# A bidirectional Mamba layer on one core: scan inputs in three PSUM banks, convolution two units ahead, one list position per scan

## What is computed

```python
xz = jnp.einsum('ed,bld->bel', in_proj_w, hidden_states)
out_f = _mamba_dir(xz, ...)
out_b = _mamba_dir(xz[:, :, ::-1], ...)[:, :, ::-1]
return jnp.einsum('bdl,od->blo', out_f + out_b, out_proj_w)
...
# _mamba_dir, 256 channels d, 16 states n, 512 positions l
u = _causal_conv_silu(x, conv_w, conv_b)
x_dbl = jnp.einsum('bdl,kd->bkl', u, xproj_w)
delta = jax.nn.softplus(jnp.einsum('dr,brl->bdl', dtproj_w, x_dbl[:, :r]) + dt_bias)
dA = jnp.exp(jnp.einsum('bdl,dn->bdln', delta, A))
dBx = jnp.einsum('bdl,bnl,bdl->bdln', delta, Bm, u)
h = _ssm_scan(dA, dBx)
y = jnp.einsum('bdln,bnl->bdl', h, Cm) + Dp * u
return y * silu(z)
...
# ffn: Hadamard transform, 4-bit quantization per token, ternary weight
xq = _quantize_activations(xn @ H)
return jnp.einsum('bsi,oi->bso', xq, _ternary_quantize_ste(weight))
```

## Time and profile before

| | |
|---|---|
| runs | 977.39, 978.01, 972.45 us; median 977.39 |
| profiled execution | 976.08 us, span of its instructions 974.0 us |
| mean granted TensorE clock | 0.864 of 2.4 GHz |
| DMA | 72.5 MB, mean 74 GB/s |
| POOL, states by C | 256 times, mean 2365 ns |
| DVE, scans | 512 times, mean 1202 ns |
| ACT, decays | 512 times, mean 710 ns |

### The profile page before, as it was taken

The page is one execution under the profiler, slowest core; times in us unless marked ns, Lnnn a source line. Parts: engine busy times, 40 slices in busy tenths (PEclk is TensorE's granted clock), DMA queues, the critical chain, the costliest instruction groups (busy, mean ns, idle before and its releaser), DMA issues.

```text
span 974.0 us, 13835 instructions
## 1 busy us (share of the span) xinstructions
PE 765.9 (79%) x3873; PEld 384.4 (39%) x3873; DVE 800.2 (82%) x838; ACT 782.1 (80%) x1454; POOL 750.2 (77%) x454
## 2 busy tenths in 40 slices
PE   3486977689786977979689697878978697797994
PEld 1233443343433435334353344434443343433452
DVE  2278988898788878888888887889878887897995
ACT  2599995899878987789967998589986898878970
POOL 2159887788768977789787887878886798777994
PEclk9788988889787988979889797988978798897797
DMA  3424225070620607024070512507052070702400
GB/s 91 113 66 118 48 79 107 4 163 4 141 55 30 135 3 172 24 70 91 30 166 3 126 38 70 124 3 162 3 126 68 10 154 3 172 14 68 95 7 27
DMA packets 51433, 72.53 MB, mean 74 GB/s; under 512 B 6704, under 2 KB 19920, under 8 KB 51408
## 3 DMA queue, kind: packets, MB, share of 16 engines
q1 hardware_dynamic: 50976, 71.97, 31.6%
q10 hardware_dynamic: 432, 0.26, 0.1%
HBM read 60.68 MB, written 11.53 MB: 74 GB/s over the span
## 4 chain that ended last, share of the span: by engine, by line
POOL 29%; issue 27%; PE 18%; ACT 15%; DVE 8%; DMA 2%; POOLq 1%; SPq 0%; DVEq 0%; ACTq 0%
POOL hst L678 22%; PE pb L792 5%; DVE hst L569 5%; ACT da L416 4%; POOL dbx_t L688 4%; PE b_ps L879 4%; ACT dbx_t L405 2%; PE y L894 2%; PE b_ps L864 1%; PE y L891 1%; POOL t_log L694 1%; ACT xn L308 1%; PE pb L856 1%; DVE b_ps L557 1%; PE pb L811 1%
## 5 line engine op out<-in xcount | busy, mean ns | idle before, releaser
L678 POOL TENSOR_TENSOR hst<-hst,c_rep 128x1024 f32<-128x1024 f32 x256 | 600.6, 2365 | 170.8 <-DVE hst L569 170.1
L569 DVE TENSOR_TENSOR_SCAN hst<-da,b_ps 128x512 f32<-128x512 f32 x512 | 586.3, 1202 | 43.1 <-ACT da L416 21.4
L879 PE MATMUL b_ps<-ident,dbx_t 128*128 128x128 f32 x1536 | 246.6, 301 | 158.3 <-DVE hst L569 157.4
L416 ACT ACTIVATE da<-rep,neg_a 128x511 f32<-128x511 f32 x512 | 336.2, 710 | 5.8 <-DVE hst L569 3.8
L879 PEld LDWEIGHTS b_ps<-ident,dbx_t 128*128 128x128 f32 x1536 | 181.0, 151 | 281.2 <-DVE hst L569 255.7
L405 ACT ACTIVATE dbx_t<-du_t,b_t 128x256 f32<-128x256 f32 x576 | 247.0, 496 | 2.5 <-PE b_ps L879 1.7
L894 PE MATMUL y<-hst,sum_sel 128*32 128x512 f32 x1024 | 148.9, 657 | 3.0 <-POOL hst L678 3.0
L792 PE MATMUL pb<-xnt,conv_wt 128*128 128x512 f32 x256 | 121.0, 617 | 0.8 <-ACT xnt L316 0.8
L688 POOL TENSOR_TENSOR dbx_t<-du_t,b_t 128x1024 f32<-128x1024 f32 x48 | 91.3, 1903 | 2.7 <-ACT du_t L388 2.7
L864 PE MATMUL b_ps<-t_log,spread_sel 32*128 32x512 f32 x256 | 73.4, 679 | 14.3 <-POOL t_log L740 9.8
L557 DVE TENSOR_TENSOR b_ps<-b_ps,b_rep 128x1024 f32<-128x1024 f32 x64 | 78.0, 1219 | 5.4 <-PE b_ps L864 5.4
(11 more groups left out here) (111 smaller groups left out, 588.5 us busy)
## 6 DMA issues: line engine op xcount, KB each, us to landing
rep<-d_scr SPq DMA_DIRECT2D x128, 256.0 KB, 9.1
c_rep<-bc_scr SPq DMA_DIRECT2D x64, 256.0 KB, 4.8
d_scr<-t_pos SPq DMA_DIRECT2D x15, 512.0 KB, 3.0
b_rep<-bc_scr SPq DMA_DIRECT2D x64, 64.0 KB, 2.2
x_ln<-x SPq DMA_DIRECT2D x8, 256.0 KB, 3.3
x_res<-x SPq DMA_DIRECT2D x8, 256.0 KB, 2.8
out<-x_res SPq DMA_DIRECT2D x8, 256.0 KB, 7.1
conv_wt<-conv_w SPq DMA_DIRECT2D x2, 512.0 KB, 5.8
```

The costliest lines, as they stand in the source:

```text
L416: nc.scalar.activation(da[s % 2][:, j, 1:L], rep[d][h][:, j, 1:L], ACT.Exp, scale=neg_a[:, d, h, j, q:q + 1]).then_inc(decay_done, 1)
L569: nc.vector.tensor_tensor_scan(hst[s % RING][:, j, :], da[s % 2][:, j, :], b_ps[:, j, :], 0.0, ALU.mult, ALU.add).then_inc(scan_done, 1)
L678: nc.gpsimd.tensor_tensor(hst[s % RING][:, two, :], hst[s % RING][:, two, :], c_rep[d][:, q:q + 1, :].broadcast_to([P, 2, L]), ALU.mult).t ...
L879: ins = tr(b_ps[:, j, P * c:P * (c + 1)], dbx_t[(NX * d + q - 1) % 2][:, c, NJ * h + j, :, :].rearrange("p r e -> p (r e)"), ident[:, :])
```

## The change

- `b_ps` has three banks instead of four, and scan g (counted through all units) uses bank g mod 3; `pb` has three instead of two. PE issues the input of scan k+3 as soon as scan k is done.
- The lists of all engines go scan by scan: PE, DVE and ACT have a position per scan k, with side work behind it. Copies are issued one at a time instead of in pairs, and `times_b` works on one bank, a scan ahead.
- The convolution for W goes tap by tap behind the inputs of positions 8, 9, 10, 12 (half 0) and 16, 17, 20, 21 (half 1) of unit U. The sigmoids are at ACT's positions 17 and 27, `make_u` at DVE's 16 and 23, so u for W is made in unit U. x_proj for V is at PE's positions 0 and 1. `log_error`, `correction` and `delta` are behind scans 9, 10, 11; before, they were around scans 14 and 15.
- All batches are written out; the hardware loop and its registers are gone. The prologue makes unit 1's u and normalizes batch 1 as well.
- The quantized activations go into `x_ln` instead of `xn`, and x is loaded two batches ahead, behind the rep loads. B and C are spread before delta is stored. The token scale is computed on DVE instead of POOL; x_proj and `steps` use 64 columns or rows once; z_proj reads `xnt_kept`.

The core of the diff:

```diff
+G = NJ * SLOTS
+UNITS = 2 * NB
+BANKS = 3
+CONV_BANK = (2, 0)
...
-        b_ps = ps("b_ps", [P, NJ, L])
+        b_ps = ps("b_ps", [P, BANKS, L])
         y = ps("y", [P, NH, L])
-        pb = ps("pb", [P, 2, L])
+        pb = ps("pb", [P, 3, L])
...
             def load_x(b):
-                src = rows(x, b)
-                wait(sp, xn_ready, b)
-                sp.dma_start(x_ln[:, :, :], src).then_inc(x_loaded, DMA)
+                wait(sp, xn_ready, b - 1)
+                wait(sp, xqt_filled, b - 2)
+                sp.dma_start(x_ln[:, :, :], rows(x, b)).then_inc(x_loaded, DMA)
...
+            def spread(V):
+                d = V % 2
+                store_bc(V)
+                load_bc(V)
                 sp.wait_ge(delta_ready, V + 1)
                 sp.dma_start(d_scr[d].rearrange("h p l -> p h l"), t_pos[:, :, :]).then_inc(delta_stored, DMA)
-                load_bc(d, V)
                 sp.wait_ge(delta_stored, DMA * (V + 1))
                 for h in range(NH):
                     load_delta(d, h)
...
+            for U in range(UNITS):
+                b, d = divmod(U, 2)
+                if U < UNITS - 1:
+                    spread(U + 1)
+                if d == 0 and b + 2 < NB:
+                    load_x(b + 2)
+                if d == 1 and b > 0:
                     store_out(b - 1)
+                    load_res(b)
...
+                wait(act, scan_done, G * U + k - 2 * NJ + 1)
+                nc.scalar.activation(da[s % 2][:, j, 1:L], rep[d][h][:, j, 1:L], ACT.Exp, scale=neg_a[:, d, h, j, q:q + 1]).then_inc(decay_done, 1)
...
+                for k in range(G):
+                    decay(U, k)
...
+                    if k == 5 and nxt:
+                        keep_xdbl(V)
...
+                    if k in (8, 9) and nxt:
+                        softplus_in(V, k - 8)
+                    if k == 10 and nxt:
+                        keep_bt(V)
+                        softplus_exp(V)
+                    if k == 11 and nxt:
+                        softplus_one(V)
+                    if k == 12:
                         if nxt:
+                            softplus_log(V)
+                        if d == 1 and b + 2 < NB:
+                            log_var(b + 2)
+                            guess_rstd(b + 2)
...
+                    if k == 17:
+                        if conv:
+                            u_sigmoid(W, 0)
+                        inputs_free(U, 3, 2 * U + 2)
+                        inputs_t(U, 3, 0)
+                    if k in (18, 19, 20):
+                        inputs_t(U, 3, k - 17, whole=k == 20)
+                    if k == 22 and d == 1 and b + 2 < NB:
+                        normalize(b + 2, x_ln)
+                    if k == 23 and nxt:
+                        keep_dut(V, 0, 2 * V + 1)
+                    if k == 25 and nxt:
+                        inputs_free(V, 1, 2 * V + 1)
+                        inputs_t(V, 1, 0)
+                    if k == 26 and nxt:
+                        keep_dut(V, 1, 2 * V + 2)
+                        inputs_t(V, 1, 1)
+                    if k == 27 and conv:
+                        u_sigmoid(W, 1)
...
+                    if k + 1 < NH * NJ:
+                        times_b(U, k + 1)
+                    if k == G - 1 and nxt:
+                        times_b(V, 0)
+                    scan(U, k)
+                    if k == 2 and d == 0 and b > 0:
+                        gate_y(b - 1, 0)
+                    if k == 5 and d == 0 and b > 0:
                         gate_y(b - 1, 1)
+                    if k == 9 and nxt:
+                        log_error(V)
+                    if k == 10 and nxt:
+                        correction(V)
+                    if k == 11 and nxt:
                         delta(V)
+                    if k == 16 and conv:
+                        make_u(W, 0)
+                    if k == 20 and d == 0 and b + 2 < NB:
+                        statistics(b + 2, x_ln)
+                    if k == 23 and conv:
+                        make_u(W, 1)
...
+                wait(pe, scan_done, g - BANKS + 1)
+                mm(b_ps[:, g % BANKS, :], spread_sel[at, :], du[at, s, :], start=True, stop=True).then_inc(t_filled, 1)
...
+                    if k + BANKS < G:
+                        inputs(U, k + BANKS)
                     elif nxt:
+                        inputs(V, k + BANKS - G)
+
+                    if k in (0, 1) and nxt:
+                        pe.wait_ge(u_ready, 2 * V + 2)
+                        if d == 0:
+                            wait(pe, xq_ready, b)
                         else:
+                            pe.wait_ge(dut_ready, 2 * U + 2)
+                        x_proj(V, k)
...
+                    if k == 4 and nxt:
                         if d == 0:
+                            pe.wait_ge(xnt_ready, min(b + 2, NB))
                         else:
+                            pe.wait_ge(gate_ready, 2 * b + 2)
+                        steps(V, 0)
+                    if k == 5 and nxt:
                         if d == 0:
+                            wait(pe, xqt_ready, b)
                         else:
+                            pe.wait_ge(gate_ready, 2 * b + 1)
+                        steps(V, 1)
+                    if k == 6 and nxt:
+                        b_transposed(V, pb[:, 2, :])
+                    if k % NJ == NJ - 1 and k > NJ:
+                        sum_states(U, k // NJ - 1)
+                    if k in (8, 9, 10, 12) and conv_next:
+                        pe.wait_ge(bt_ready, V + 1)
+                        pe.wait_ge(xnt_ready, W // 2 + 1)
+                        conv(W, 0, ((8, 9, 10, 12).index(k),))
+                    if k in (13, 14):
+                        skip_product(U, k - 13)
+                    if k in (16, 17, 20, 21) and conv_next:
+                        pe.wait_ge(delta_ready, V + 1)
+                        conv(W, 1, ((16, 17, 20, 21).index(k),))
+                    if k == 18 and nxt:
+                        pe.wait_ge(delta_ready, V + 1)
+                        du_transposed(V, 0)
```

More of the change, by code:

```diff
@@ L78, in build @@
         qinv = sb("qinv", [P, NC])
-        xq = xn
+        xq = x_ln
         xqt = sb("xqt", [P, L])
@@ L178, in wait @@
         def wait(eng, s, count):
-            if not isinstance(count, int) or count > 0:
+            if count > 0:
                 eng.wait_ge(s, count)
-        def batches(eng, body):
-            body(0)
-            with eng.Fori(1, NB - 1) as i:
-                body(i)
-            body(NB - 1)
-        def first(b):
-            return isinstance(b, int) and b == 0
-        def last(b):
-            return isinstance(b, int) and b == NB - 1
         @block.sync
@@ L241, in spread @@
                     load_delta(d, h)
-            load_x(0)
+            sp.dma_start(x_ln[:, :, :], rows(x, 0)).then_inc(x_loaded, DMA)
             for d in range(2):
@@ L498, in _ @@
+            for U in range(UNITS):
+                unit(U)
             keep_xqt(NB - 1)
@@ L582, in _ @@
-            statistics(0)
+                nc.vector.tensor_tensor(x_res[:, :, :], pb[:, 1, :].rearrange("p (c o) -> p c o", c=NC), x_res[:, :, :], ALU.add).then_inc(out_ready, 1)
+            statistics(0, x_ln)
             for n in range(2):
@@ L785, in _, with conv @@
             tr = nc.tensor.transpose
-            def conv(d, V, h, taps, free, count):
-                wait(pe, free, count)
+            def conv(V, h, taps):
+                d = V % 2
                 for k in taps:
@@ new lines, in inputs, with skip_product @@
+                wait(pe, scan_done, g - BANKS + 1)
+                for c in range(NC):
+                    ins = tr(b_ps[:, g % BANKS, P * c:P * (c + 1)], dbx_t[(NX * d + q - 1) % 2][:, c, NJ * h + j, :, :].rearrange("p r e -> p (r e)"), ident[:, :])
+                ins.then_inc(t_filled, 1)
+            def skip_product(U, h):
+                d = U % 2
+                step = slice(None, None, -1 if d else 1)
+                pe.wait_ge(u_ready, 2 * U + 2)
+                mm(y[:, h, :], skip[:, d, h, :], u[d][:, h, step], start=False, stop=False, skip_group_check=True)
@@ L887, in sum_states @@
                     wait(pe, y_read, 2 * b - 1 + h)
-                if s == SKIP_AT - 1:
-                    pe.wait_ge(u_ready, 2 * (2 * b + d) + 2)
-                    for n in range(NH):
-                        mm(y[:, n, :], skip[:, d, n, :], u[d][:, n, step], start=False, stop=False, skip_group_check=True)
                 pe.wait_ge(prod_done, 2 * S + 2)
@@ L919, in _ @@
-            du_transposed(0, 1, delta_ready, 1)
-            conv(1, 1, 0, range(TAPS), dut_ready, 1)
-            conv(1, 1, 1, range(TAPS), dut_ready, 2)
+            x_proj(0, 1)
+            steps(0, 0)
+            steps(0, 1)
+            b_transposed(0, y[:, 1, :])
+            pe.wait_ge(first_du, 1)
+            for k in range(BANKS):
+                copy(0, k)
+            pe.wait_ge(delta_ready, 1)
```

(9 more changed lines are left out.)

703 lines of the change are left out of this document (313 added, 390 removed).

## The result

The changed kernel takes 1238.95 us (four runs, 1234.29 to 1241.11) against 977.67: 1.268 times as long, 95% interval 1.263 to 1.274. Forecast were 1031 us, range 968 to 1080. The direction was right, the size was not. The profiled execution has a span of 1232.7 us, at a mean granted clock of 0.75 instead of 0.864.

What follows compares the result with a forecast made beforehand. Hand-overs between engines, no engine filling the span, were taken as the bound. Start 82, intervals 7 x 58.2 and 7 x 63.6, late x 13, end 88.5, less 7 gave 1029 us, with 2.1 around it 1031; range 968 to 1080.

Steps and rivals of the forecast that it cites:

- Smaller items: Minor effects across engines: single copies, three banks and POOL's work called hidden; removed registers and branches save 0.5 us per interval.
- the sum: Whole run: start 82, seven intervals each of 58.2 and 63.6, late x 13, end 88.5, minus 7: 1029 us of span.
- first L: L is a unit's first correction of the logarithm on DVE; the run's first was placed at 82 us, before at 78.2.
- Half clock over the copies: Rival, k=0 to 5: PE idles at k=23, stays at 1.2 GHz; two steps cost 3 to 4 us a unit, 1075; chance 0.07.
- second stall at `make_u`: Behind scan 23, DVE waits for half 1's sigmoid: about 6 us in a forward unit, 8 in a backward one.
- the wait at `log_error`: DVE waits there for ACT's logarithm 4.6 us a unit instead of 2.7, about 65 us in all.
- Half 0's sigmoid: ACT sees the convolution's half 0 finished at L+9.9, after waiting 5.5 us at this first sigmoid.
- the wait for x: At k=20, statistics waits for x loaded behind the rep loads, delaying the sigmoid 2.2 us; six forward units, 13 us.
- credit of 7 us for the removed registers: Loop's register arithmetic and branches gone: 0.5 us saved per interval, 7 us in all, bounds 0 and 14.
- the faster rival: ACT reaches the second sigmoid in time, stalls at make_u sum below about 6 us a pair; 920 or 940 us; chance 0.17.
- the ring: Engines pass four moved things round each unit; ACT waits for a tap behind scan 12; intervals 58.2 and 63.6 us.
- ACT then bound by its own: Variant of the faster rival: ACT limits at 49 us a unit plus waits of 5, intervals 54 and 57, 940 us.

Runs made afterwards that it cites:

- e1: The changed kernel with du copies at full height: 128-row selection weights, zero outside the 32 rows that select, and all 128 rows of du; 1064.78 us.
- p1: A separate kernel computing nothing of the layer: PE issues nine stretches of fp32 matmuls without waits, each after a rest of about 16 us; its time is no comparison.
- e4: e1 with ACT's second sigmoid behind decay 23 instead of 27; 1059.96 us.
- e5: e4 with x of batch b+2 loaded ahead of the B, C and delta spreads instead of behind the rep loads; 1044.29 us.
- e6: e5 with log_error, correction and delta behind scans 12, 13, 14 instead of 9, 10, 11, and make_du one POOL slot later; 989.13 us.
- e11: e6 with first sigmoid and its make_u at 18, backward second du_t copy behind decay 24, softplus chain and keep_xdbl later on ACT; 943.44 us.

## Why the prediction went wrong, step by step

**The step that failed** stands under "Smaller items": "in k=0 to 5 a step is copy plus projection, 1.8, against DVE's 1.12 + 0.6 = 1.7, hidden while the clock is full". The clock is not full there: the step takes 3.9 us at 0.50, DVE waits 119.8 us for copies, and e1 shows the price, 174 us, 84% of the miss of 208. By the terms of the sum: 14 intervals of 74.8 instead of 61.3 are 189 us; first L 87.9 instead of 82 and end 97.7 instead of 88.5 are 15; in e1 these two are 82.3 and 90.3. The last 4 are the distance from the profiled execution to the median.

**The rival was on the list, but with the wrong price and cause.** "Half clock over the copies" had chance 0.07 and 3 to 4 us a unit, "two such steps". It costs 11.5 us an interval (74.8 - 63.3), and 13 us more in the beginning and the end: the low clock covers not two steps but 32 us, from the last copies of one unit over projection, sums and steps to the taps of the next. Its cause was wrong too: the prediction let the idle time at k=23 lower the clock and any work raise it again. Idle time does lower it (from the second on, each stretch of p1 starts at 0.50 behind its rest of 16 us, and 642 to 644 above is at 0.50), but it is back at 1.00 before the copies, and p1 shows matmuls that never raise it. And the evidence against it, at 560 to 562, was of transposes and state sums, which p1 shows at 1.00; it said nothing of 32-row matmuls. The window from 562 to 582 of the same trace holds 32-row copies at 1.00, but in pairs and beside taps, and single copies could not be read from it either. The Trainium skill ("TensorE: Matmul & The Clock Gate", "Part 4: PE-mode transpose") has it that the full clock does not engage for transposes; the fp32 transposes of p1, with 1.00 from 315 to 321, do not agree, and the trace decides.

**What held.** With the clock restored (e1) the sum can be judged. First L 82.3 (82), end 1058.6 - 968.3 = 90.3 (88.5), total 1064.8 (1031): 34 us off, 3%, with no term wrong by more than 4 us a unit. So the direction was not luck: with the full clock the changed kernel is still 1.091 times the one before. But the prediction put most of the loss on the second stall at `make_u`, and taking the waits away one after the other gives 5 us for that stall (e4), 16 for x (e5) and 55 for the wait at `log_error` (e6). Half 0's sigmoid starts at L+8.4 in the changed kernel (predicted 9.9; the clock was already full there), the second is done at L+26.8 (predicted 28.2, backward):

```profile
619.89 0.69 ACT L325 ACTIVATE t_exp<-pb,half_bias 128x512 f32<-128x512 f32 x1 [3.81 <-PE pb L819]
...
637.65 0.63 ACT L327 ACTIVATE t_exp<-t_exp 128x512 f32<-128x512 f32 x1
```

DVE stalls 5.75 us at `make_u` in this backward unit (8) and 6.13 in the forward unit behind it (6). The 99 us in all seem to meet the 80 to 100 forecast, but 22.6 of them are four waits of the prologue; the 14 stalls meant are 76.4. ACT waits 3.8 at the first sigmoid (5.5).

**What was mis-sized.** The wait at `log_error` was 4.6 to 4.9 a unit and 72.7 in all in e1 (4.6 and 65), but 6.30 and 94.5 in the changed kernel, since the steps run at half clock. x costs 16 us (13). Forward intervals of e1 took 63.8 us on the mean (60.3 to 66.1), where 58.2 and 1.9 for x were summed; backward ones 62.8 for 63.6. In the forward one of the window above, the wait for x and the one at `make_u` each leave PE at 1.2 GHz for some us behind them (0.81 on the mean from 590 to 634); that this is the cause was read from the trace, not tested. The credit of 7 us for the removed registers can't be seen by itself, and its base was thin: inside the loop the forward intervals of the kernel before alternate between 53.7 and 55.1 us, and the prediction set the first interval, 53.0, against one of 55.1.

**The deciding point of the faster rival** was that the two stalls at `make_u` must shrink. e4 shrank them by 53 us and the time fell by 5 at most: the ring has several late places in a row, and the loss goes to the next. The part of that rival that was true is that the lists could hide it: e11 reaches 943, near the 940 that the prediction gave for "ACT then bound by its own", but only with full-height copies, x in time and ACT's chain rearranged. None of that is in the change as made.

**Open.** Single copies with taps beside them were not tried, and pairs without taps only in p1, where they began at 0.50 and stayed there. So it isn't shown which of the two kept the clock at 1.00 in the kernel before.
